# Spike attention's product with the values: whole array, or two TensorE tiles of 64 rows

## What is computed

```
def _L0_attn_ref(x, ...):                      # x: (32, 32, 512)
    Q, K, V = (sigmoid(4 * (batchnorm(x @ W) - 1)) for W in (Wq, Wk, Wv))
    t_Q = 1 - Q.mean(-1, keepdims=True)
    t_K = 1 - K.mean(-1, keepdims=True)
    delta_t = t_Q - swapaxes(t_K, 1, 2)         # (32, 32, 32)
    f = 0.9 * exp(-abs(delta_t) / 0.5)
    A = where(delta_t < 0, f, -f) + 0.9
    return A @ V @ Wo + bo
x = x + attention(layernorm(x))
```

## Time and profile before

| | |
|---|---|
| median of three runs | 753.13 us |
| the profiled execution | 753.35 us |
| its span | 751.6 us |
| TensorE busy | 712.2 us, 95% |
| VectorE busy | 486.9 us, 65% |
| ScalarE busy | 440.0 us, 59% |
| stage of the change (first spike product to last gate product) | 552.0 to 599.1 us |

### The profile page before, as it was taken

The page is one execution under the profiler, slowest core; times in us unless marked ns, Lnnn a source line. Parts: engine busy times, 40 slices in busy tenths (PEclk is TensorE's granted clock), DMA queues, the critical chain, the costliest instruction groups (busy, mean ns, idle before and its releaser), DMA issues.

```text
span 751.6 us, 13998 instructions
## 1 busy us (share of the span) xinstructions
PE 712.2 (95%) x4845; PEld 594.2 (79%) x4845; DVE 486.9 (65%) x883; ACT 440.0 (59%) x957; POOL 240.4 (32%) x208
## 2 busy tenths in 40 slices
PE   4899999999999999999999989999999759999996
PEld 3677888888888888888888877888788747888875
DVE  6766766675757666757576666966467655555573
ACT  4655675675756756856566566565654324665560
POOL 1462212121212121212121226734930013555535
PEclk9999999999999999999999999999999859999999
DMA  9941121212121212121212306640134572666658
GB/s 296 108 127 42 44 85 43 85 55 71 51 74 42 84 42 84 44 82 47 78 42 85 99 2 182 194 143 0 57 113 144 193 251 63 111 111 111 113 74 332
DMA packets 59671, 75.19 MB, mean 100 GB/s; under 512 B 8784, under 2 KB 33360, under 8 KB 59632
## 3 DMA queue, kind: packets, MB, share of 16 engines
q1 hardware_dynamic: 52032, 58.16, 26.0%
q0 software_dynamic: 4720, 11.27, 8.3%
q10 hardware_dynamic: 2880, 5.24, 1.9%
HBM read 54.75 MB, written 19.92 MB: 99 GB/s over the span
## 4 chain that ended last, share of the span: by engine, by line
PE 84%; DVE 7%; ACT 3%; DMA 3%; issue 2%; POOL 1%; SPq 0%; POOLq 0%; ACTq 0%; DVEq 0%
PE pK L32 41%; PE pV L32 11%; PE pP L32 9%; PE pV L1574 5%; PE pT L1475 4%; PE pT L1663 4%; PE pS L1618 2%; PE pP L1645 2%; PE pT L1781 1%; DMA fin<-total 1%; PE pT L1455 1%; PE pS L1735 1%; DVE bst L968 1%; DMA total<-big,idx 1%; PE pS L1802 1%
## 5 line engine op out<-in xcount | busy, mean ns | idle before, releaser
L32 PE MATMUL pK<-parts 128*128 128x512 f32 x840 | 211.3, 399 | 1.6 <-POOL parts L555 1.6
L32 PEld LDWEIGHTS pK<-parts 128*128 128x128 f32 x840 | 152.0, 188 | 32.3 <-POOL parts L555 2.0
L515 POOL TENSOR_TENSOR parts<-big,parts 128x1024 fp32r<-128x1024 f32 x32 | 77.8, 2430 | 311.5 <-ACT parts L741 311.5
L1010 DVE TENSOR_TENSOR kn<-pK,head_rs 128x512 f32<-128x512 f32 x62 | 42.9, 692 | 58.3 <-ACT head_rs L655 58.3
L32 PE MATMUL pK<-w,lhs 128*128 x276 | 70.6, 405 | 1.6 <-DVE lhs L1392 1.6
L32 PEld LDWEIGHTS pK<-w,lhs 128*128 128x128 f32 x276 | 51.2, 192 | 12.8 <-issue 2.7
L1408 DVE TENSOR_TENSOR w_p<-big,w_p 128x1024 fp32r<-128x1024 f32 x22 | 26.9, 1225 | 39.7 <-ACT w_p L925 39.7
L32 PE MATMUL pP<-pT,parts 128*128 128x256 f32 x384 | 52.0, 284 | 0.0
L1004 DVE TENSOR_REDUCE head_ss<-sq 128x8 f32<-128x512 f32 x62 | 42.5, 685 | 13.1 <-ACT sq L649 13.1
L589 POOL DMA_INDIRECT big<-x_rows,idx_x x23 | 25.6, 1112 | 78.3 <-DVE idx_x L1382 62.6
L649 ACT ACTIVATE sq<-pK 128x512 f32<-128x512 f32 x62 | 36.9, 595 | 23.1 <-PE pK L32 23.1
(11 more groups left out here) (306 smaller groups left out, 1454.5 us busy)
## 6 DMA issues: line engine op xcount, KB each, us to landing
big<-in_ctx_dram SPq DMA_DIRECT2D x32, 512.0 KB, 3.8
total<-zero SPq DMA_DIRECT2D x32, 256.0 KB, 3.9
w_raw<-in_L_ffn_w_dram SPq DMA_DIRECT2D x16, 512.0 KB, 6.2
big<-in_L_ffn_w_dram SPq DMA_DIRECT2D x8, 512.0 KB, 7.4
fin<-total SPq DMA_DIRECT2D x8, 512.0 KB, 7.3
x_rows<-big ACTq DMA_DIRECT2D x8, 256.0 KB, 2.1
total<-big ACTq DMA_DIRECT2D x8, 256.0 KB, 2.3
big<-in_x_dram SPq DMA_DIRECT2D x1, 1536.0 KB, 10.5
```

Of the source, the lines that this page charges most:

```text
L32: last = pe.matmul(out, lhs(a, c), rhs(b, c), start=start and c == first and n == 0, stop=stop and c == chunks - 1 and n == 2)
L515: nc.gpsimd.tensor_tensor(ctxN[:, u, LO], ctx_raw[:, u], ctxN[:, u, HI].bitcast(F32), ALU.subtract).then_inc(cn_lo, 1)
L1010: tt(heads(kn[:, t]), heads(pKV[t][:, :]), per_head(head_rs[:, t]), ALU.mult).then_inc(k_n, 1)
```

## The change

The product of a tile is issued as eight matmuls in place of four. For each chunk c there is one for each half i of the tile's tokens: 64 rows of V as weights (all 128 columns of the chunk), 64 moving columns, on the half of the array that has those rows (`tile_position=(i * HD, 0)`, HD = 64). Half i writes columns 0 to 63 of each chunk in bank i, so every tile writes both banks. ScalarE and VectorE take a tile in two instructions of 256 columns, one for each bank, and put them together in `lhs2`. The semaphores av_hi and av_lo count two for a tile. self_product(s) waits for the whole eviction of tile s-1, self_product(0) has the wait for z_c that tile 1 had, and a nop stands between the waits and the matmuls. The old names of the two banks go on as `pXT` for the transposes of the preamble, without any other change to them.

```diff
-        pAV = (pP[:, :, :].rearrange("p t n -> p (t n)").rearrange("p (c n) -> p c n", c=C),
+        pXT = (pP[:, :, :].rearrange("p t n -> p (t n)").rearrange("p (c n) -> p c n", c=C),
                pV1[:, :].rearrange("p (c n) -> p c n", c=C))
+
+        pAV = [bank[:, :, 0:HD] for bank in pXT]
+        tok_half = lambda i: slice(i * HD, (i + 1) * HD)
...
                 act.wait_ge(av_mm, t + 1)
                 if t >= 2:
                     act.wait_ge(ao_mm, t - 1)
-                act.activation(lhs2[:, t % 2, HI], pAV[t % 2], ACT.Copy).then_inc(av_hi, 1)
+                for i in range(2):
+                    act.activation(lhs2[:, t % 2, HI, :, tok_half(i)], pAV[i], ACT.Copy).then_inc(av_hi, 1)
...
             def self_low(t):
-                dve.wait_ge(av_hi, t + 1)
-                tt(lhs2[:, t % 2, LO], pAV[t % 2], lhs2[:, t % 2, HI].bitcast(F32), ALU.subtract).then_inc(av_lo, 1)
+                for i in range(2):
+                    dve.wait_ge(av_hi, 2 * t + i + 1)
+                    tt(lhs2[:, t % 2, LO, :, tok_half(i)], pAV[i], lhs2[:, t % 2, HI, :, tok_half(i)].bitcast(F32),
+                       ALU.subtract).then_inc(av_lo, 1)
...
             def self_product(s):
                 pe.wait_ge(z_sig, 2 * TILES + s + 1)
-                if s == 1:
+                if s == 0:
                     pe.wait_ge(z_c, 3 * TILES - 2)
-                if s >= 2:
-                    pe.wait_ge(av_lo, s - 1)
+                else:
+                    pe.wait_ge(av_lo, 2 * s)
+                pe.nop(nofuse=True)
                 for c in range(C):
-                    last = pe.matmul(pAV[s % 2][:, c, :], v_self[:, s, c * P:(c + 1) * P], dt_all[:, s, :],
-                                     start=True, stop=True)
+                    for i in range(2):
+                        last = pe.matmul(pAV[i][:, c, :], v_self[tok_half(i), s, c * P:(c + 1) * P], dt_all[tok_half(i), s, tok_half(i)],
+                                         start=True, stop=True, tile_position=(i * HD, 0))
                 last.then_inc(av_mm, 1)
...
-                    pe.wait_ge(av_lo, t + 1)
+                    pe.wait_ge(av_lo, 2 * t + 2)
```

More of the change, by code:

```diff
@@ L700, in _ @@
                     act.wait_ge(rem_pe, 1)
-                    act.activation(remT[:, :, :], pAV[0], ACT.Copy).then_inc(rem_act, 1)
+                    act.activation(remT[:, :, :], pXT[0], ACT.Copy).then_inc(rem_act, 1)
                 if t in (3, 4):
                     act.wait_ge(ctx_t, t - 2)
-                    act.activation(ctxT[:, 0, HI, :, (t - 3) * P:(t - 2) * P], pAV[4 - t], ACT.Copy).then_inc(ctx_hi, 1)
+                    act.activation(ctxT[:, 0, HI, :, (t - 3) * P:(t - 2) * P], pXT[4 - t], ACT.Copy).then_inc(ctx_hi, 1)
                 if t == 5:
@@ L728, in _ @@
                     act.wait_ge(rem_pe, 3)
-                    act.activation(kT_rem[:, :, :], pAV[0][:, :, 0:B], ACT.Copy).then_inc(rem_act, 1)
+                    act.activation(kT_rem[:, :, :], pXT[0][:, :, 0:B], ACT.Copy).then_inc(rem_act, 1)
                     keys_copy(1)
@@ L1080, in _ @@
                     part = slice((t - 3) * P, (t - 2) * P)
-                    tt(ctxT[:, 0, LO, :, part], pAV[4 - t], ctxT[:, 0, HI, :, part].bitcast(F32),
+                    tt(ctxT[:, 0, LO, :, part], pXT[4 - t], ctxT[:, 0, HI, :, part].bitcast(F32),
                        ALU.subtract).then_inc(ctx_lo, 1)
@@ L1514, in _ @@
                     for c in range(C):
-                        last = pe.transpose(pAV[0][:, c, :], rem_raw[:, c * P:(c + 1) * P], ident[:, :])
+                        last = pe.transpose(pXT[0][:, c, :], rem_raw[:, c * P:(c + 1) * P], ident[:, :])
                     last.then_inc(rem_pe, 1)
@@ L1522, in _ @@
                     for c in range(C):
-                        last = pe.transpose(pAV[4 - t][:, c, :], ctx_raw[:, 0, t - 3, c * P:(c + 1) * P], ident[:, :])
+                        last = pe.transpose(pXT[4 - t][:, c, :], ctx_raw[:, 0, t - 3, c * P:(c + 1) * P], ident[:, :])
                     last.then_inc(ctx_t, 1)
@@ L1541, in _ @@
             for c in range(C):
-                last = pe.transpose(pAV[0][:, c, :], kn_x[:, 2, c * P:(c + 1) * P], ident[:, :])
+                last = pe.transpose(pXT[0][:, c, :], kn_x[:, 2, c * P:(c + 1) * P], ident[:, :])
             last.then_inc(rem_pe, 1)
```

## The result

The changed kernel is slower: 760.03 us (median of seven runs, 757.19 to 760.98) against 753.74 for the kernel before in the same session (seven runs, 753.05 to 756.28); the ratio of after to before is 1.0063, with an interval of 1.0048 to 1.0077. So about 4.7 us are lost (0.0063 x 753.7), between 3.6 and 5.8. The forecast of 755.8 us, a loss of 2.7, lies under that interval, and 760.03 lies outside the range of 754.3 to 757.8. The profiled execution took 760.24 us, span 758.5, against 753.35 and 751.6.

The account below looks back on a forecast made before the run. The prediction took TensorE, busy for 95% of the span, as the bound. It added 1.0 + 2 x 0.35 + 4 x 0.24 = 2.7 us to reach 755.8 us, with an 8-in-10 range of 754.3 to 757.8.

Parts of the forecast that it names:

- Loads go by columns, tiles side by side: Spike product: a weight load's time follows its columns, 0.111 us each, while two row tiles load at once.
- (a): Rival: tiles run one after the other, 16 loads at 0.111 us, +6.2 us, 762 us; chance 4%.
- (b): Rival: loads of half the rows take half the time, 753.1 us, no change; chance 8%.
- (c): Rival: the spike product halves and the mode-change drain is hidden, 751.0 us, faster; chance 3%.
- Entering and leaving the mode: Tile-mode drain around each spike product: net +0.35 us at tiles 2 and 3, +0.24 at tiles 4 to 7.
- (f): Rival: nop and mode switch cost half of the 0.35 us for row tiles, 755.0 us; within the 82% main case.
- The wait at tile 1: Tile 1's product must wait for `self_low(0)`, delaying the first projection by 0.95 to 1.03 us, taken as 1.0.
- (d): Rival: the wait on `self_low` binds in every step, +3 us over six steps, 758.8 us; chance 3%.
- ScalarE's and VectorE's halves: Evictions split into 256-column copies: 0.38 us each on ScalarE, 0.41 on VectorE, ending up to 0.1 us earlier.
- the sum: 1.0 us at tile 1, 2 x 0.35 and 4 x 0.24 us for tiles 2 to 7: 2.7 us, all on the chain.
- (e): TensorE's half-clock edge behind the stage may shift either way, some 1.4 us, 754.4 or 757.2; within the 82% main case.
- After the stage everything hangs on its end and moves along: Routing, gathers and experts shift with the stage's end, adding no loss of their own.

Follow-up runs that it names:

- e5: Changed kernel with four 64x64 tiles and two pairs of banks taking turns: 754.61 us, ratio 0.9999 to the kernel before.
- e11: Changed kernel repeated without any edit, a single run: 757.11 us, with no half-clock stretch in the first projection.
- e7: Changed kernel without the nop between the waits and the tiled matmuls: 759.56 us, ratio 1.0065 to the kernel before.
- e3: Kernel before with one edit, each product waiting for the whole eviction of the previous tile, no row tiles: 757.33 us, ratio 1.0028.
- e1: Changed kernel repeated without any edit: 761.66 us against 755.38 for the kernel before, ratio 1.0082.
- e9: Changed kernel repeated without any edit, a single run: 758.24 us.
- e14: Changed kernel with 100 nops that left no instruction in the profile, so in effect a repetition: ratio 1.0048 to the kernel before.
- e6: Changed kernel with four 64x64 tiles and still a single pair of banks: 755.46 us, ratio 1.0022 to the kernel before.
- e10: Kernel before repeated without any edit, a single run: 753.73 us.
- e12: Kernel before repeated without any edit, a single run: 752.95 us.
- e13: Kernel before with 65 nops that left no instruction in the profile, so in effect a repetition: ratio 1.0004.
- e17: Kernel before with 33 tiny unused matmuls (66 records) behind the router's last merge: 756.31 us, ratio 1.0011.
- e4: Changed kernel with its two banks doubled, so a product waits for tile s-2 again: 757.97 us, ratio 1.0042 to the kernel before.
- e16: Four 64x64 tiles with doubled banks, plus 65 nops that left no instruction, in effect a repetition: ratio 0.9998 to the kernel before.
- e18: Four 64x64 tiles with doubled banks, plus 66 tiny unused matmuls (132 records): 753.61 us, ratio 0.9982 to the kernel before.
- e2: Changed kernel with six unused matmuls filling the idle time ahead of tile 1's product: 757.47 us, ratio 1.0030 to the kernel before.
- e15: Changed kernel with the six filling matmuls, plus 100 nops that left no instruction, in effect a repetition: ratio 1.0035 to the kernel before.
- e8: Kernel before with four unused matmuls in its own idle time before the first projection: 754.78 us against 754.49, ratio 1.0001.

## Why the prediction was wrong, step by step

**Loads go by columns, tiles side by side: right, both.** 188 ns for 64x128, 0.11 from pair to pair, pairs 0.01 apart. Rivals (a), 16 loads one after another, and (b), half the rows for half the time, are out by this, and (c), faster, by the step. e5 tested the same rule from its other side: 64 columns, 0.06 from round to round, and a step that is 0.43 us shorter. The Trainium skill, "TensorE: Matmul & The Clock Gate", section "LDWEIGHTS (loading the stationary operand)", has this rule, and these durations bear it out.

**Entering and leaving the mode, +0.24 and +0.35: right.** The steady step grew by 0.25 us. For all six steps on the chain the forecast had 1.66; e11 shows 2.56 - 0.88 = 1.68, so rival (f), a cheaper change of mode, is out. e7 adds that this is the price of the change of mode and not the nop's, as "TensorEngine Tiling (Array Packing)" of the Trainium skill, Key Properties, has it, which gives no figure.

**The wait at tile 1, +1.0: right.** 1.01 with the old evictions (e3), 0.88 with the halved ones (e11); the forecast had up to 0.1 between these two. In later steps no wait for `self_low` opened, so rival (d) is out. ScalarE's and VectorE's halves are 0.36 to 0.39 and 0.41 us against 0.38 and 0.41 in the forecast.

Up to here the sum was 2.7, and 2.56 was measured (e11). What failed is the clock, taken as an edge that might move either way, and the way behind the stage, taken as nothing.

**(e), the clock: wrong.** The prediction read one fall of the clock in the trace of before, took it as an edge that might lie somewhat earlier or later, and let it give or take 1.4 us. But a new stretch can open where there was none, and that only costs. The place was in the prediction's own text: the same sentence that moved the product of tile 1 out of the idle time left TensorE with 1.35 us of idle time ahead of a thin product, where it had been 0.89 ahead of a full projection. In four of six profiles of the changed kernel, one of them without its nop (after, e1, e9, e7, not e11 and e14), a stretch fell on the first projection, at 1.6 us. It also stands in e3 (1.91 us of idle time), not in e6 (1.72), and never where the idle time is 1.1 us or less (before, e10, e12, e13, e17, e4, e5, e16, e18) or filled (e2, e15, e8). At this place the direction should have been one-sided: before had 1.00 there, so there was clock to lose and none to win. The edge behind the stage, which the prediction did price, moved as well: it is the 1.4 us of the first slot in after, a size that (e) had right, but in e1 and e7 it cost nothing. Why most of the changed kernel's executions in the first two sessions have over 35 us at half clock, and so how much of the whole loss the filled idle time takes away (4.2 us in one session, 0.4 in another), is not settled.

**"After the stage everything hangs on its end and moves along": wrong by 0.7 to 0.8 us.** The change made TensorE's program longer by 64 records and their weight loads. Its last packet of instructions then came among the last transfers, and the additions at the end of the kernel took longer. Only the place is shown, and the time that goes with it; which transfer the packet held up was not followed. e17 does this to the kernel before, e18 undoes it for e5. The page of before lists its 23 packets; that another program length moves them was not asked.

**The sum as the runs have it.** 2.56 for steps and wait, 1.6 in four of six profiles, which is 1.1 on average, and 0.7 at the end: 4.4 us, against 4.7 (3.6 to 5.8) by the ratio of the first session, 6.2 by e1 and 3.6 by e14. The mean of the three is 4.85. The place of the long stretch adds 0.3 on average (half of 6.87 - 6.26, six profiles against four), less than it scatters. The medians alone (760.03 against 753.74) differ by 6.3; four of the changed kernel's seven executions in that session were of those with over 35 us at half clock (four of six in e1's, two of five in e14's), and the loss is smaller where they are fewer.

**What would beat both** is e18: four tiles of 64x64 with the banks doubled and the program's length such that its packets come ahead of the last transfers, 0.9982 (0.9972 to 0.9992) of before. That is 1.4 us (0.6 to 2.1), and its stage is shorter by 1.06 us. But e5 and e16, whose stage is as short, stand level with before, with the packet among the last transfers; and the packets' place will move with the next edit.

## What to carry to other kernels

A row tile saves nothing where the weight loads set the pace and keep their columns; split the columns too, or leave it. When an edit opens idle time on TensorE ahead of dense work, put a one-sided loss for its clock into the sum (here 1.6 us for 1.35 us of idle time, in four of six profiles), and try it with unused matmuls in the hole: if more work makes the kernel faster, look at the granted clock before and after. And when an edit makes a program longer, look where the last packets of its instructions fall.

## What the runs showed of the hardware

Idle time of 1.34 to 1.91 us ahead of a product of some 1 us came before a stretch of 3.4 us at 0.50 (after, e1, e9, e7, e3), but not every time: e11 with 1.37 us, e14 with 1.31 and e6 with 1.72 kept 1.00. So the idle time alone does not decide, and one profile of such a kernel doesn't settle it. The same kernel without any edit shows a 3.4 us stretch near 447 us in some executions (e13) and none in others (before, e10, e12), and that alone is 1.4 us.

The long stretch behind the stage lasted 27.3 us in sixteen of twenty profiles, 30.7 in three (after, e8, e17) and 23.9 in e3. TensorE's work inside it took twice its time: the first slot's length goes by how much of it lies there, 9.89 us (5.03 of it at 0.50, e10) to 12.01 (9.19, e18).

A packet of 16 KB on the instruction queue took 0.9 to 1.4 us, and with it among the last transfers the end of the kernel took 0.7 us longer. The Trainium skill, "Runtime: NRT & Kernel Launch", section "Instruction fetch mechanics", has it that instructions are fetched in blocks of 16 KiB and calls the cost of crossing from one to the next mostly hidden. These runs show a cost that it does not name: the 0.7 us came not to TensorE, whose instructions they were, but to GpSimd, which waited for the transfers.

Changing into and out of tiles costs 0.10 us ahead of the first load (0.21 from load to load in place of 0.11) and 0.20 behind the last matmul (the next one ends 0.43 us later, 578.76 to 579.19 in after, in place of 0.23); the first of these is the same with and without a nop, and four 64x64 tiles gave a product of 0.69 us where the whole array took 1.14 as the timeline counts it.
